# Causal attention on one core: the masked copy of the values moved one step later, two roundings written as products with ones

## The reference

```python
qkv = jnp.einsum('sbh,oh->sbo', ln1_out, qkv_weight)   # S = 32 places, B = 128 sequences, H = 128
scores = jnp.einsum('sbhd,tbhd->bhst', q, k) * scale   # 16 heads of 8, 4 key/value heads
scores = jnp.where(causal, scores, jnp.finfo(scores.dtype).min)
probs = jax.nn.softmax(scores, axis=-1)
attn = jnp.einsum('bhst,tbhd->sbhd', probs, v).reshape(S, B, H)
proj_out = jnp.einsum('sbh,oh->sbo', attn, proj_weight)
```

## Time and profile before

| | |
|---|---|
| median of 3 runs | 852.64 us (851.43 to 855.21) |
| profiled execution | 857.17 us, its span 855.3 us |
| TensorE clock granted, mean | 0.927 of 2.4 GHz |
| busy share of the span | PE 84%, DVE 72%, ACT 49%, POOL 25% |
| the 32 steps of the causal attention | 490.9 to 632.5 us of the span |

### The profile page before, as it was taken

One profiled execution on the slowest core, in us unless ns is written; L12 is line 12 of the kernel. 1 busy time (PEld: TensorE's weight loads), 2 busy tenths in 40 slices (PEclk: granted clock), 3 DMA queues, 4 the chain that ended last, 5 costly groups with the idle time before them and its releaser, 6 DMA issues. The chain is left out here.

```text
span 855.3 us, 25351 instructions
## 1 busy us (share of the span) xinstructions
PE 720.1 (84%) x9696; PEld 526.7 (62%) x9696; DVE 614.5 (72%) x1802; ACT 418.2 (49%) x777; POOL 218.1 (25%) x327
## 2 busy tenths in 40 slices
PE   3459988889797999998996488778759999999997
PEld 2335555555465767776774255556537888888886
DVE  7567887877777888888872688777555666666653
ACT  3022333223243777776664356656425455554553
POOL 3344222332428133431001734331011111011100
PEclk9968999899796999999997699999969999999999
DMA  4000000041035122222200000000000000000000
GB/s 104 9 18 18 23 21 21 23 96 21 12 84 128 54 63 74 74 77 70 82 15 13 0 5 4 5 4 5 4 3 1 14 12 5 8 12 12 12 13 13
DMA packets 33078, 26.36 MB, mean 31 GB/s; under 512 B 9740, under 2 KB 29912, under 8 KB 32984
## 3 DMA queue, kind: packets, MB, share of 16 engines
q1 hardware_dynamic: 29944, 24.07, 10.7%
q10 hardware_dynamic: 3040, 0.98, 0.5%
HBM read 13.51 MB, written 7.34 MB: 24 GB/s over the span
## 5 line engine op out<-in xcount | busy, mean ns | idle before, releaser
L1964 PEld LDWEIGHTS bank<-w2r,hme 128*128 128x128 f32 x1024 | 132.6, 192 | 15.8 <-ACT hme L1909 1.4
L1964 PE MATMUL bank<-w2r,hme 128*128 128x128 f32 x1024 | 135.8, 276 | 0.0
L1909 ACT ACTIVATE hme<-bank,b 128x512 f32<-128x512 f32 x128 | 86.5, 687 | 97.7 <-PE bank L104 97.7
L1933 DVE SCALAR_TENSOR_TENSOR Xq<-bank,wgte,Xq 128x128 f32 (+1 forms) x256 | 72.1, 343 | 52.6 <-PE bank L1964 39.8
L1096 DVE TENSOR_REDUCE mx<-bank 128x4 f32<-128x512 f32 x128 | 87.9, 688 | 24.9 <-PE bank L1141 23.4
L1014 ACT ACTIVATE P<-bank 128x512 f32<-128x512 f32 x128 | 76.5, 600 | 15.3 <-PE bank L1162 14.0
L530 ACT ACTIVATE w2r<-bank 128x512 f32<-128x512 f32 x40 | 23.9, 597 | 115.4 <-PE bank L843 85.2
L1089 DVE TENSOR_SCALAR P<-P 128x512 f32<-128x512 f32 x128 | 61.3, 479 | 3.1 <-ACT P L1014 3.0
L102 PE MATMUL bank<-xTe,w 128*128 (+1 forms) x128 | 49.2, 385 | 5.4 <-PEq L1328 5.4
L1739 POOL TENSOR_SCALAR rs<-mv 128x4 f32<-128x4 f32 x8 | 1.6, 194 | 203.4 <-DVE mv L1801 203.4
L854 PE MATMUL bank<-w_raw,hm 128*128 128x128 f32 x320 | 49.1, 303 | 2.8 <-DVE X L768 2.4
(11 more groups left out here) (384 smaller groups left out, 1779.3 us busy)
## 6 DMA issues: line engine op xcount, KB each, us to landing
cross_q<-qh SPq DMA_DIRECT2D x24, 128.0 KB
Q<-cross_q SPq DMA_DIRECT2D x8, 384.0 KB, 4.1
X<-in_x SPq DMA_DIRECT2D x8, 256.0 KB, 2.8
Xq<-X SPq DMA_DIRECT2D x32, 64.0 KB
cross_k<-kh SPq DMA_DIRECT2D x16, 128.0 KB
Yq<-Y SPq DMA_DIRECT2D x32, 64.0 KB
out_x<-Xq SPq DMA_DIRECT2D x32, 64.0 KB
cload<-in_ctx SPq DMA_DIRECT2D x8, 192.0 KB, 2.6
```

The costliest lines, as they stand in the source:

```text
L1909: act.activation(hm[:, p % HR], UP[p % RING][:], ACT.Gelu_apprx_tanh, bias=b1[:, p:p + 1]).then_inc(s["gelu"], 1)
L1933: last = dve.scalar_tensor_tensor(x, Y[f % 2][:, 128 * i:128 * i + 128], w, x, ALU.mult, ALU.add)
L1964: last = pe.matmul(Y[f % 2][:, cols], hm[:, p % HR, cols], w2r[:, p], start=(p % 2 == 0 and i == 0), stop=(p % 2 == 1), skip_group_check=True)
```

## The change

The copy of the values out of VM is made for step q in step q, behind the maxima of q+1 and ahead of the slots, where it was made for step q+1 behind the slots. Its wait is now for `pv_done >= q - 1`, the product of two steps before. TensorE's program has the same instructions in the same order and the same semaphore values. The two roundings (maxima to bf16, reciprocals to f16) become products of the number with a tile of ones, where they were copies with a change of type.

```diff
-                        dve.tensor_copy(m2[:, 0:16], mx[:]).then_inc(s["m_hi"], 1)
+                        dve.tensor_tensor(m2[:, 0:16], mx[:], ones[:, 0:16], ALU.mult).then_inc(s["m_hi"], 1)
                         dve.wait_ge(s["m_hi"], q + 3)
                         dve.tensor_tensor(m2[:, 16:32], mx[:], m2[:, 0:16], ALU.subtract).then_inc(s["m_lo"], 1)
+                    if has(q):
+                        dve.wait_ge(s["v_psum"], q + 1)
+                        after(dve, s["pv_done"], q - 1)
+                        dve.tensor_tensor(Vq[q % 2][:], VM[:, 0:128].rearrange("p (a x) -> p a x", a=4),
+                                          gm[:].unsqueeze(1).broadcast_to([128, 4, NG * HD]), ALU.mult
+                                          ).then_inc(s["v_ready"], 1)
                     if chunk(n + 1):
                         for i in ((0, 1), (2, 3), (4,), ())[k]:
                             slot(n + 1, i)
-                    if has(q + 1):
-                        dve.wait_ge(s["v_psum"], q + 2)
-                        after(dve, s["pv_done"], q)
-                        dve.tensor_tensor(Vq[(q + 1) % 2][:], VM[:, 0:128].rearrange("p (a x) -> p a x", a=4),
-                                          gm[:].unsqueeze(1).broadcast_to([128, 4, NG * HD]), ALU.mult
-                                          ).then_inc(s["v_ready"], 1)
...
-                        dve.tensor_copy(Dh[0][:], dr).then_inc(s["dd_hi"], 1)
+                        dve.tensor_tensor(Dh[0][:], dr, ones[:, 0:2 * T].rearrange("p (a s) -> p a s", s=T), ALU.mult
+                                          ).then_inc(s["dd_hi"], 1)
```

## The result

The changed kernel takes 858.83 us (median of 7 runs, 853.91 to 859.11) where the kernel before takes 853.00 (7 runs, 850.75 to 855.21). The medians lie 5.8 us apart. The ratio on record, from all the runs, is 1.0046, 95% interval 1.0025 to 1.0067: 2.1 to 5.7 us more. The profiled execution of the changed kernel was its lowest run (853.91 us, span 852.0); its step 1 begins at 489.42 us, that of before at 494.33, though the parts ahead are the same. So spans are not compared here but stretches inside this part. Lines after L1521 stand a few further down in the changed kernel: the copy is L1525, `high` L1611, the product L1619 and L1624, the transpose L1642, the scores L1645 and L1654.

The account below looks back on a forecast made before the run. No engine is full; waits between engines set the pace. 2.37 + 0.4 - 0.4 = 2.4 us longer, on 852.64 giving 855.0 us; range for 8 in 10: 850.0 to 861.0.

Parts of the forecast that it names:

- fetch rival: TensorE's instruction fetch moves with the wait at `high`, so "issue" waits hide nothing: 861.5 us; chance 0.24.
- Place 3: Steps 3, 7, ..., 27: `high` starts 0.93 us later; step 3 pays 0.93, steps 7, 19, 23 0.48 each: 2.37.
- swallowed 0.45: Step 20, transpose to scores: 1.12 us where 0.67 is least; the 0.45 above takes up half of the 0.93.
- Place 2: Steps like 18: `high` starts 0.72 us later, covered by TensorE's 0.97 us wait for ScalarE's exponential; cost 0.
- Place 1: Step of each group where `widen` comes on top of the slot products ahead of `high`; cost 0.
- Place 0: Step of each group with six slot products ahead of `high`: 0.07 us late, 0.4 in six groups.
- What the lost wait gives: TensorE's waits for VectorE at `rest` and `widen` shrink: 0.4 us gained, 0 of `widen`'s 2.7 counted.
- The roundings: VectorE's casts made products: worth 0 on the path by either end, whether or not GpSimd's add holds them.
- VectorE's lead reaches TensorE: Faster rival: TensorE's waits at `widen` and `rest` go, 2.7 + 0.5, the new wait finds slack: 849.4 us; chance 0.12.

Follow-up runs that it names:

- e8: The changed kernel with the copy ahead of the maxima in places 0, 1 and 2, behind them in place 3 alone; ratio to before 1.0033.
- e1: The kernel before with only the two roundings as products with ones, the copy in its old place; 852.98 us against 851.49, ratio 1.0018.
- e2: The changed kernel with the copy of step q ahead of the maxima of q+1, products with ones kept; 851.69 us against 851.49, ratio 1.0011.
- e6: The kernel before with three buffers for the masked copy in place of two; 851.38 us against 851.49, ratio 1.0009.
- e7: The changed kernel with the copy ahead of the maxima in place 3 alone, behind them in the other places; ratio to before 1.0019.
- e4: The changed kernel with the two roundings as casts again, so the move alone; 854.37 us against 851.49, ratio 1.0037.
- e9: e2 with one of ScalarE's casts of the keys in place 2 moved to VectorE; 854.59 us against 855.50 for before, ratio 0.9979.

## Why the prediction was right, and where it was off

Forecast +2.4 us; measured 2.1 to 5.7. The direction, the mechanism and the main place are right; the sum is at the lower end. The median of 858.83 us lies in the range of 850.0 to 861.0, but above the forecast's own band (853.2 to 857.5) and inside that of the fetch rival (857 to 862), which the runs reject. That the range held is in part luck: its upper end was there for that rival.

- **Place 3**, the main term (2.37 us): e8, which has this wait alone, lies above the mean of before, e1, e2 and e6 by 0.77 in steps 1 to 5, 0.45, 0.32 and 0.47 in the others, together 2.01. Forecast were 0.93 and three times 0.48. `high` came 1.40 and not 1.52 us after the scores, since the copy starts before the subtraction has ended (573.40 against 573.31 + 0.17), where I had put a gap. The swallowed 0.45 is right: the wait for the copied maxima went from 0.67 us to 0.23 in the same place.
- **Place 2**, forecast 0.72 late and worth nothing: 0.60 late, and worth nothing (e7's 16.66 with it, e8's 17.14 without it).
- **Place 1**, forecast 0: the step that failed. I took place 3's times from the scores to the copy for every place. In this one GpSimd's add holds a rounding on VectorE's way to the copy, that of the reciprocals ahead of the maxima in steps 5 and 9 and that of the maxima themselves in step 1, and I had followed the add only as far as `widen`. The wait is 0.40 to 0.51 us in steps 1, 5 and 9. With the longer wait of place 2 behind it, it makes 17.39 - 17.12 (e8) = 0.27 of the stretch from 5 to 9, and nothing of that from 1 to 5 (17.01 and 17.04).
- **Place 0**, forecast 0.4 in all: no wait at `high` in steps 4, 8, 12, 16, 20 and 24. **What the lost wait gives**, forecast 0.4 out of 3.2: nothing, by e6 and e2. That these two errors cancel is luck.
- **The roundings**, forecast 0 by either end: 0 in the steps of e1. The open point, whether a product is held, is settled for the add: 0.96 us beside L1357, and 0.66 for the maxima's rounding in step 1. The Trainium skill's rule (SBUF — State Buffer, Who interferes with whom) holds here; the root L1342, beside which L1521 ran in 0.18 us, stays an exception, in the changed kernel too: 0.17 us at 573.31.
- **The fetch rival** falls. That the "issue" waits are waits for instructions, which the prediction only supposed, the traces bear out: the twelve of them have 138 such waits of TensorE of over 0.2 us between 490 and 640 us, and each ends 1.2 to 1.7 us after a packet of the instruction queue q8 has landed (in the earlier trace rows at 612.79 and 617.19, behind packets landed at 611.50 and 615.81). Steps 11, 27 and 28 wait at `high`, and their "issue" waits shrink or go. In the lines of the product they sum to 10.2 + 2.9 = 13.1 us before, 3.8 + 0.6 = 4.4 in the changed kernel and 3.4 in e4, but 9.5 in e1, 12.7 in e2 and 12.3 in e6. In steps 27 to 30 the changed kernel waits 5.0 us at `high` and 0.7 in the product; before waited 6.8 in the product. A wait at `high` covers the fetch, as the forecast had it; that this cover is whole for each step can't be read from stretches that scatter so.
- **VectorE's lead reaches TensorE** falls by e2 and e6.

The four clean stretches of the changed kernel sum to 68.53 us, 2.2 over the mean of 66.3 for the four kernels that keep the old steps. By the measured ratio the change costs 3.9. What the other 1.7 are, if they are anything (the interval begins at 2.1, and the medians differ by 5.8), was not found. A second bank for the values, so that `high` need not wait for the copy at all, was not tried.

## What to carry to other kernels

A large wait on an engine that others do not wait for is worth nothing by itself: taken away at one line it comes up at the next. When a copy that frees a buffer is moved behind other work, ask what the writer of that buffer waits for, place by place, and start from when that engine is really free, not from when its input is there. Where the path goes through a third engine, moving its work (here one cast of 0.63 us) gave more here than reordering the two that wait for each other.

## What the runs showed of the hardware beyond that

A cast of 32x512 f16 to f16 takes 0.29 us on VectorE and 0.63 on ScalarE (587.84 in e9 above; 587.05 there for ScalarE's).

TensorE's granted clock fell in the last group of the changed kernel, in a stretch in which the engine was busy 2.42 of 4.00 us. From 608 us (stretch and its us; busy us of PE, PEld, DVE, ACT and POOL; granted clock; DMA share; GB/s):

```profile
608.00:612.00 4.00, 2.42 (x122) 2.03 (x123) 1.33 (x5) 1.14 (x3) 0.00 (x0) 0.89 0.01 4
612.00:616.00 4.00, 3.03 (x125) 2.51 (x124) 1.83 (x6) 1.19 (x2) 0.00 (x0) 0.50 0.03 8
616.00:620.00 4.00, 3.26 (x85) 2.63 (x83) 2.82 (x8) 0.86 (x2) 0.00 (x0) 0.76 0.00 0
```

0.50 is 1.2 of 2.4 GHz; a product of 128x512 at 611.76 takes 0.63 us where the same at 571.96 takes 0.38. In the profile of before the clock there is 1.00, but e1, e2 and e6, whose time is that of before, also show stretches of 0.55 to 0.8. From step 1 to 645 us the lower level lasts 20.5 us in the changed kernel and in each of these three, 16.4 in before and 13.7 in e4, so it is not the change's.
